# Second layer of a decoder kernel: GpSimd adds the exponentials of each pair of key tiles, and TensorE multiplies the sums of pairs with ones

## The chip, the core and the metric

The kernel runs on one core of a Trainium2 chip. Of its engines five matter here: TensorE (PE; its weight loads are shown as PEld) multiplies, VectorE (DVE) and ScalarE (ACT) empty PSUM and do the elementwise work, GpSimd (POOL) can work on SBUF beside them, SyncE (SP) issues transfers. The metric is the device time of one launch in microseconds (us), the median of several runs.

## The reference, cut to what matters

Three layers follow each other: attention with quantised numbers, cross attention, and attention with experts. Only the second is touched. There 16 sequences of 224 rows look at a context of 750 rows each, with 16 heads of 32 columns:

```python
q = (Q @ Wq + bq).reshape(B, L, H, E)
k = (K @ Wk + bk).reshape(B, S, H, E)
v = (V @ Wv + bv).reshape(B, S, H, E)
scores = jnp.einsum('blhe,bshe->bhls', q, k)
A = jax.nn.softmax(scale * scores, axis=-1)
out = jnp.einsum('bhls,bshd->blhd', A, v).reshape(B, L, H * E)
return out @ We + be
```

The softmax needs, for each row and head, the sum of the exponentials over all 750 keys.

## The kernel before, in words

The second layer handles one sequence (a "batch", `NB` = 16) after another, and in it four groups of four heads (`NG2` = 4, `GH` = 4). The 750 keys are six tiles of 125 (`MC`), taken as three pairs (`TP` = 3). For group g and pair t the work is a ring over four PSUM banks:

- `scores(u, g, t)`: TensorE writes the scores of two key tiles, four heads and 224 rows, keys on the partitions; the second half of it adds minus the row maximum.
- ScalarE's exponential `S.activation(prob[:, t, ...], ...)` (L1348) turns 1792 scores per partition into `prob`.
- `row_max(m, u, g, i)`: TensorE writes a quarter of the scores of the NEXT group into the same four banks, rows on the partitions, and VectorE's `reduce_max` (L1375) takes their maximum. Only then may the next `scores` write there (`r_free`).
- `values(u, g, t)`: TensorE multiplies `prob` with v and, in the other half of the same PSUM bank, with ones, which gives the sums of exponentials (L1239). Four heads stand side by side in the array, each in 32 of its columns.

After the third pair VectorE's `attend` takes the reciprocal of the sums and multiplies (L1387, L1388). `combine` (L1380 to L1382) turns the four maxima of the next group into the bf16 numbers that the small transposes of unit M (L1147) need, and M must be done before the first `scores` of the next group.

Between these steps TensorE fills its time with the dense work of the next batch, by the table `SLOTS`: slot 2t+1 lies behind `scores(t)`, slot 2t+2 behind `row_max(t+1)`, slot 0 at the group's start. Slot 4 is empty in groups 1, 2 and 3. In group 0 the units are transposes of the context (C) and the output product (O) of the batch before; in groups 1 to 3 they are the q, k and v products (Q, K, VV; L1137 to L1139). The order of a group on TensorE is: `row_max` 0 of the next group, M, slot 0, then for t = 0, 1, 2: `scores`, slot, `row_max` t+1, slot, `values`. Each engine runs its own program in order and waits on semaphores; the first and the last batch are written out, the fourteen between are a loop of seven rounds of two batches. GpSimd only adds the bias `be` to the rows of each batch (L1130). In the last batch there is no dense work left except O.

Of the kernel before, what the change touches and what calls it, by code (L numbers as in the profile page):

```python
# [6 lines left out]
F32 = mybir.dt.float32  # L7
# [5 lines left out]
ALU = mybir.AluOpType  # L13
# [8 lines left out]
NB, NS, D = 16, 224, 512  # L22
# [6 lines left out]
NCTX, MT = 750, 6  # L29
MC = NCTX // MT  # L30
H2, DH2 = 16, 32
# [44 lines left out]
def decoder_kernel(nc, a, out):  # L76

    V, S, G, PE = nc.vector, nc.scalar, nc.gpsimd, nc.tensor
    ctx = ExitStack()
    with ctx:  # L80
        arenas = []

        def open_arena(name, size, st):
            arenas.append((st.enter_context(nc.sbuf_tensor(name, [P, size // 4], F32)), {"low": 0, "high": size}))
            st.callback(arenas.pop)

        def own(name, shape, dt=F32, st=ctx):

            return st.enter_context(nc.sbuf_tensor(name, shape, dt))
# [23 lines left out]
        def ps(name, shape, dt=F32, st=ctx):  # L113
            return st.enter_context(nc.psum_tensor(name, shape, dt))
# [18 lines left out]
        ones = own("ones", [P, P])  # L133
# [8 lines left out]
        psum = ps("psum", [P, 8, D])  # L142
# [796 lines left out]
        L2 = ExitStack()  # L939
        SCALE2 = 1.0 / math.sqrt(DH2)  # L940
        GH = P // DH2
        NG2 = H2 // GH
        NK = NCTX + 2
        HC = NK // 2
        TP = MT // 2
# [2 lines left out]
        Wl = {n: own(f"W{n}_rest", [P, KC, D], F32R, L2) for n in "qkv"}  # L948
        ctxT_h, ctxT_l = (own("ctx_T_" + n, [P, KC, NK], F32R, L2) for n in ("high", "rest"))
        x1T_h, x1T_l = (own("x1_T_" + n, [P, KC, NS], F32R, L2) for n in ("high", "rest"))  # L950
        open_arena("arena_2", 122 * 1024, L2)
        We = sb("We", [P, KC, D], F32, L2)
        bias = sb("bias_qk_by_partition", [P, 2, NG2], F32, L2)
        bvT = sb("bias_v_by_partition", [P, KC], F32, L2)
# [12 lines left out]
        vR = sb("v_rows", [MC, 2, MT, D], F32, L2)  # L967
# [37 lines left out]

        ctx_r = sb("ctx_rows", [MC, MT, D], F32, L2)
        prob = sb("exps_by_key", [MC, TP, GH, 2 * NS], F32, L2)


        C, Q, K, VV, O, M = "ctx", "q", "k", "v", "out", "max"  # L1010
# [33 lines left out]
            return ORDER[at], 1  # L1044

        with phase(nc, "x2", "c", "x", "y0", "y1", "yb", "cmm", "chi", "clo", "qmm", "qmv", "kmm", "kmv", "vmm", "vmv", "rmm", "rfr", "nmx", "tmm", "tmv",
                   "smm", "exp", "avm", "att", "omm", "ord", "dch", "st") as (
                ctx_in, x_in, y_in0, y_in1, y_ready, c_mm, c_high, c_rest, q_mm, q_moved, k_mm, k_moved, v_mm, v_moved, r_mm, r_free, nmx_ready, t_mm, t_moved,
                s_mm, exp_done, av_mm, attended, o_mm, o_read, dch, r2_out), nc.Block() as block:
            y_in = (y_in0, y_in1)  # L1050

            def loop(eng, first, body, final):
# [9 lines left out]
            def y_count(b, u):  # L1062
                return b * 8 + (16 if u == 0 else 8)

            def score_psum(n, cols):
                return psum[0:n, 0:GH, 0:cols]
# [57 lines left out]
            @block.gpsimd  # L1124
            def _(pool):
                with pool.Fori(0, NB // 2) as pair:
                    for u in range(2):
                        b = pair * 2 + u
                        pool.wait_ge(y_in[u], y_count(b, u))
                        G.tensor_tensor(y2[:, u, :, :], y2[:, u, :, :], be[:, :].unsqueeze(1).broadcast_to([HALF, 2, D]), ALU.add).then_inc(y_ready, 1)  # L1130

            @block.tensor
            def _(pe):
# [98 lines left out]
                def values(u, g, t):  # L1232
                    for s in range(2):
                        mt = 2 * t + s
                        for to in range(2):
                            for j in range(GH):
                                h = g * GH + j
                                lhsT = vR[:, u, mt, h * DH2:(h + 1) * DH2] if to == 0 else ones[0:MC, 0:DH2]
                                last = PE.matmul(psum[DH2 * j:DH2 * (j + 1), 6 + g % 2, to * NS:(to + 1) * NS], lhsT, prob[:, t, j, s * NS:(s + 1) * NS],  # L1239
                                                 start=(mt == 0 and to == 0), stop=(mt == MT - 1 and to == 1))  # L1240
                    last.then_inc(av_mm, 1)

                def body(b, u, first, last):
                    b_next, b_before = b + 1, b - 1 if not first else None
                    for g in range(NG2):
                        n = b * NG2 + g
                        more = not (last and g == NG2 - 1)
                        g_r, u_r = (g + 1) % NG2, u if g < NG2 - 1 else 1 - u

                        def slot(i):  # L1250
                            for what in SLOTS[g][i]:
                                dense(what, b, b_next, b_before, u, first, last)

                        def next_max(i):
                            if not more:
                                return
                            if i == 0:
                                pe.wait_ge(q_moved, n + 2)
                                pe.wait_ge(k_moved, n * 2 + 4)
                                pe.wait_ge(r_free, n * 4 + 4)  # L1260
                            else:
                                pe.wait_ge(exp_done, n * TP + i)
                            row_max(n + 1, u_r, g_r, i)

                        def next_scores(t):
                            if more:
                                pe.wait_ge(r_free, n * 4 + (4 + t + 1))
                            elif t == 0:
                                pe.wait_ge(r_free, n * 4 + 4)
                            else:  # L1270
                                pe.wait_ge(exp_done, n * TP + t)
                            if t == 0:
                                pe.wait_ge(t_moved, n + 1)
                            scores(u, g, t)

                        def next_values(t):
                            if t == 0:
                                pe.wait_ge(attended, n + 1)
                                if g == 0:
                                    pe.wait_ge(v_moved, b * MT + MT)  # L1280
                            pe.wait_ge(exp_done, n * TP + (t + 1))
                            values(u, g, t)
                        next_max(0)
                        dense((M, g), b, b_next, b_before, u, first, last)
                        slot(0)
                        for t in range(TP):
                            next_scores(t)
                            slot(2 * t + 1)
                            next_max(t + 1)
                            slot(2 * t + 2)  # L1290
                            next_values(t)
# [12 lines left out]
                        row_max(0, 0, 0, i)  # L1304

                def final():
                    for i in range(2):
                        if i == 0:
                            pe.wait_ge(o_read, 2 * NB - 2)
                            pe.wait_ge(t_moved, NB * NG2)  # L1310
                        unit(O, i, 4 + i, NB - 1, 1)
# [3 lines left out]
            def _(act):  # L1315
# [19 lines left out]
                def body(b, u, first, last):  # L1335
                    for g in range(NG2):
                        n = b * NG2 + g

                        def slot(i):
                            for what in SLOTS[g][i]:  # L1340
                                if present(what, first, last):
                                    unit(*what, bank(what), b + 1, 1 - u)
                        unit(M, g, bank((M, g)), b, u)
                        slot(0)
                        for t in range(TP):
                            act.wait_ge(s_mm, n * TP + (t + 1))
                            act.wait_ge(av_mm, n * TP + (t + 1))
                            S.activation(prob[:, t, :, :], score_psum(MC, 2 * NS), ACT.Exp, scale=SCALE2).then_inc(exp_done, 1)  # L1348
                            slot(2 * t + 1)
                            slot(2 * t + 2)  # L1350
# [7 lines left out]
            def _(dve):  # L1358
# [24 lines left out]

                def attend(n, g, ch):

                    dve.wait_ge(av_mm, n * TP + 2 * TP)
                    ch.link(V.reciprocal(inv[:, :], psum[:, 6 + g % 2, NS:2 * NS]))  # L1387
                    V.tensor_tensor(o2T[:, g, :], psum[:, 6 + g % 2, 0:NS], inv[:, :], ALU.mult).then_inc(attended, 1)  # L1388

# [28 lines left out]

                def first():
                    dve.sem_inc(av_mm, TP)  # L1420
                    dve.sem_inc(attended, 2)
                    for i, (kind, j) in enumerate(FIRST):
                        unit(kind, j, 4 + i % 2, 0, 0)
                    for i in range(4):
                        reduce_max(0, i)
                    combine(0, Chain(dve, dch))
# [837 lines left out]
```

## Time and profile before

| | |
|---|---|
| median of 3 runs | 5535.03 us (5529.34 to 5535.2) |
| the profiled execution | 5532.44 us, its span 5530.6 us |
| TensorE busy over the span | 3949.7 us (71%) |
| VectorE, ScalarE, GpSimd busy | 2808.5 (51%), 1760.4 (32%), 250.3 (5%) |
| second layer's loop over batches | first `values` at 1625.3 us, last at 3306.5 us |

The page gives shares over three layers with different limits, so the numbers of use are those of the second layer alone. A row of the profile counts each float32 product as two matmul instructions: the 1536 products with v and the 1536 with ones appear as 3072 each. "Busy" of TensorE is time in which at least one matmul is in flight; starts that follow each other tell its pace.

### The profile page before, as it was taken

To read this page: it belongs to the slowest core of one execution; us is meant where nothing else is said; L and a number is where in the kernel's file an instruction comes from. 1 tells how busy PE (TensorE), PEld (TensorE's weight loads), DVE (VectorE), ACT (ScalarE), POOL (GpSimd) and SP (SyncE) were. 2 spreads that over 40 slices of the span, in tenths; PEclk is the share of its full clock that TensorE was granted. 3 is DMA by queue.
4 is the path that set the end of the run, shared out by engine and by line. 5 is a ranking of instruction groups with operands and counts; after the bars stand their busy time and mean duration, and the time that the engine had idled before them with its cause. 6 is when DMAs were issued, how large, how long until landed. Compare 5 with 4: busy or idle time off the path is not lost. (4 is left out here: it accounts for less than half of the span.)

```text
span 5530.6 us, 86185 instructions
## 1 busy us (share of the span) xinstructions
PE 3949.7 (71%) x31789; PEld 2779.0 (50%) x31819; DVE 2808.5 (51%) x4238; ACT 1760.4 (32%) x3704; POOL 250.3 (5%) x298
## 2 busy tenths in 40 slices
PE   0499411395069999999999972888835499999970
PEld 0234211262056666666666642555525388887860
DVE  6666988897524343344444335777773122223324
ACT  0105079782023333333333320444421122222310
POOL 0000000000000000000000000000001300000113
PEclk9999555556579999999999985999975699999985
DMA  3001423231210010001001002000001222222213
GB/s 118 0 0 48 111 76 87 78 96 62 85 51 22 23 40 27 22 23 44 22 23 38 14 5 83 0 0 0 0 0 54 85 68 68 68 68 68 71 51 129
DMA packets 156416, 266.34 MB, mean 48 GB/s; under 512 B 75824, under 2 KB 75824, under 8 KB 155264
## 3 DMA queue, kind: packets, MB, share of 16 engines
q1 hardware_dynamic: 143488, 229.39, 13.0%
q0 software_dynamic: 12672, 33.07, 2.1%
q8 instruction: 218, 3.57, 0.3%
q14 instruction: 38, 0.31, 0.0%
HBM read 165.11 MB, written 67.96 MB: 42 GB/s over the span
## 5 line engine op out<-in xcount | busy, mean ns | idle before, releaser
L1375 DVE TENSOR_REDUCE arena<-psum 112x4 f32<-112x1504 f32 x256 | 441.4, 1724 | 887.5 <-PE psum L1216 886.0
L1348 ACT ACTIVATE arena<-psum 125x1792 f32<-125x1792 f32 x192 | 320.0, 1667 | 423.9 <-PE psum L1229 423.9
L2062 PE MATMUL psum<-tokens_T_high,w_high 128*128 128x224 f32 x1280 | 357.4, 279 | 29.0 <-PE psum L2064 15.2
L543 PE MATMUL psum<-arena 64*112 64x224 bf16 x1024 | 127.2, 400 | 348.6 <-DVEq L652 261.2
L2063 PE MATMUL psum<-tokens_T_rest,w_high 128*128 128x224 f32 x1280 | 354.0, 277 | 0.0
L2064 PE MATMUL psum<-tokens_T_high,w_rest 128*128 128x224 f32 x1280 | 352.9, 276 | 0.0
L668 ACT ACTIVATE arena<-arena,scales 112x224 bf16<-112x224 int8 x512 | 286.0, 559 | 35.1 <-DVEq L653 35.0
L2140 ACT ACTIVATE arena<-psum 128x448 f32<-128x448 f32 x160 | 87.0, 544 | 633.8 <-PE psum L2064 633.8
L2181 DVE TENSOR_TENSOR gelu_T_rest<-arena,gelu_T_high 128x448 fp32r<-128x448 f32 x160 | 100.0, 625 | 369.1 <-ACT gelu_T_high L2145 369.1
L1216 PE MATMUL psum<-arena 32*112 32x376 f32 x2048 | 243.8, 532 | 60.8 <-issue 26.6
L543 PEld LDWEIGHTS psum<-arena 64*112 64x112 bf16 x1024 | 81.7, 200 | 394.2 <-DVEq L652 283.6
L2062 PEld LDWEIGHTS psum<-tokens_T_high,w_high 128*128 128x128 f32 x1280 | 248.4, 194 | 46.3 <-issue 46.3
L2062 PE MATMUL psum<-w_high,gelu_T_high 128*112 128x512 f32 x640 | 255.4, 399 | 12.4 <-PE psum L2053 11.3
L417 PE MATMUL psum<-arena 128*128 128x512 bf16 x1104 | 251.2, 383 | 13.8 <-DVEq L457 8.0
L2064 PE MATMUL psum<-w_high,gelu_T_rest 128*112 128x512 f32 x640 | 252.3, 394 | 0.0
L2063 PE MATMUL psum<-w_rest,gelu_T_high 128*112 128x512 f32 x640 | 251.9, 394 | 0.0
L2064 PEld LDWEIGHTS psum<-tokens_T_high,w_rest 128*128 128x128 f32 x1280 | 248.6, 194 | 0.0
L2063 PEld LDWEIGHTS psum<-tokens_T_rest,w_high 128*128 128x128 f32 x1280 | 248.5, 194 | 0.0
L2191 DVE COPY arena<-psum 112x512 f32<-112x512 f32 x80 | 55.3, 692 | 345.3 <-PE psum L2064 345.3
L1239 PE MATMUL psum<-arena 125*32 125x224 f32 x3072 | 224.8, 365 | 5.4 <-ACT arena L1348 5.4
L1225 PE MATMUL psum<-arena 32*125 32x224 f32 x3072 | 209.0, 388 | 19.0 <-DVE arena L1375 18.4
L1239 PE MATMUL psum<-arena,ones 125*32 125x224 f32 x3072 | 221.5, 361 | 0.0
(296 smaller groups left out, 8696.2 us busy)
## 6 DMA issues: line engine op xcount, KB each, us to landing
arena<-L_ffn_moe_w SPq DMA_DIRECT2D x16, 2048.0 KB, 12.0
arena<-arena SPq DMA_DIRECT2D x32, 896.0 KB, 6.1
arena<-ctx SPq DMA_DIRECT2D x16, 1500.0 KB
expert_rows<-arena SPq DMA_DIRECT2D x40, 448.0 KB, 3.1
arena<-x SPq DMA_DIRECT2D x2, 7168.0 KB, 22.8
arena<-x_after_attn SPq DMA_DIRECT2D x32, 448.0 KB, 15.3
dots_ints<-arena SPq DMA_DIRECT2D x16, 784.0 KB, 4.8
arena<-dots_ints SPq DMA_DIRECT2D x16, 784.0 KB, 5.6
```

The source lines that it names most:

```text
L417: last = PE.matmul(psum[:, j, :], qkvw_q[:, k, bass.ts(oc, P)], hT[:, k, j * D:(j + 1) * D], start=(k == 0), stop=(k == KC - 1))
L543: last = PE.matmul(psum[0:HALF, 4 * (hg % 2) + j, half * NS:(half + 1) * NS], stage[at, u, h // 2, half * HALF:(half + 1) * HALF], stage[a ...
L668: last = S.activation(junk[:, hg % 2, j, :], d8[:, u, h, (j % 2) * NS:(j % 2 + 1) * NS], ACT.Exp, bias=col("lowest")[0:HALF], scale=col("m ...
L1216: last = PE.matmul(psum[0:HALF, j, 0:HC], qT[rows, u, g, half * HALF:(half + 1) * HALF], kT[rows, u, g, c * HC:(c + 1) * HC], start=True, ...
L1225: PE.matmul(psum[0:MC, j, s * NS:(s + 1) * NS], kT[rows, u, g, keys], qT[rows, u, g, :], start=(s == 0), stop=False)
L1239: last = PE.matmul(psum[DH2 * j:DH2 * (j + 1), 6 + g % 2, to * NS:(to + 1) * NS], lhsT, prob[:, t, j, s * NS:(s + 1) * NS], start=(mt == 0 ...
L1348: S.activation(prob[:, t, :, :], score_psum(MC, 2 * NS), ACT.Exp, scale=SCALE2).then_inc(exp_done, 1)
L1375: return V.tensor_reduce(rmx[:, i // 2, i % 2, :], score_psum(HALF, HC), axis=AX.X, op=ALU.max).then_inc(r_free, 1)
L2062: PE.matmul(to, wh(k), xh(k), start=(k == 0), stop=False)
L2063: PE.matmul(to, wh(k), xl(k), start=False, stop=False)
L2064: last = PE.matmul(to, wl(k), xh(k), start=False, stop=(k == n - 1))
L2181: V.tensor_tensor(gTl[:, 2 * j:2 * j + 2, :], gT[:, j % 2, :, :], gTh[:, 2 * j:2 * j + 2, :].bitcast(F32), ALU.subtract).then_inc(g_rest, 1)
```

## The change

GpSimd gets new work: as soon as the exponentials of pair t are there, it adds the two key tiles of the pair into a new tile `pair2` (125 partitions x 896 floats). TensorE multiplies ones with `pair2` instead of with both halves of `prob`, in a function of its own, `sums`. It does so one step later than before: the sums of pair t stand behind the values of pair t+1, and those of the last pair stand in the next group, behind slot 0 and ahead of its first `scores`. `attend` waits for the sums. The exponential of the next group waits until GpSimd has read `prob`.

```diff
+                        for g in range(NG2):
+                            for t in range(TP):
+                                i = (b * NG2 + g) * TP + t
+                                pool.wait_ge(exp_done, i + 1)
+                                pool.wait_ge(sum_mm, i + 1)
+                                G.tensor_tensor(pair2[:, t, :, :], prob[:, t, :, 0:NS], prob[:, t, :, NS:2 * NS], ALU.add).then_inc(paired, 1)
...
-                        for to in range(2):
-                            for j in range(GH):
-                                h = g * GH + j
-                                lhsT = vR[:, u, mt, h * DH2:(h + 1) * DH2] if to == 0 else ones[0:MC, 0:DH2]
-                                last = PE.matmul(psum[DH2 * j:DH2 * (j + 1), 6 + g % 2, to * NS:(to + 1) * NS], lhsT, prob[:, t, j, s * NS:(s + 1) * NS],
-                                                 start=(mt == 0 and to == 0), stop=(mt == MT - 1 and to == 1))
+                        for j in range(GH):
+                            h = g * GH + j
+                            last = PE.matmul(psum[DH2 * j:DH2 * (j + 1), 6 + g % 2, 0:NS], vR[:, u, mt, h * DH2:(h + 1) * DH2],
+                                             prob[:, t, j, s * NS:(s + 1) * NS], start=(mt == 0), stop=False)
                     last.then_inc(av_mm, 1)
+
+                def sums(n, g, t):
+                    pe.wait_ge(paired, n * TP + (t + 1 + TP))
+                    for j in range(GH):
+                        last = PE.matmul(psum[DH2 * j:DH2 * (j + 1), 6 + g % 2, NS:2 * NS], ones[0:MC, 0:DH2], pair2[:, t, j, :],
+                                         start=False, stop=(t == TP - 1))
+                    last.then_inc(sum_mm, 1)
...
                             values(u, g, t)
+                            if t >= 1:
+                                sums(n, g, t - 1)
...
                         slot(0)
+                        if not (first and g == 0):
+                            sums(n - 1, (g - 1) % NG2, TP - 1)
...
                             act.wait_ge(av_mm, n * TP + (t + 1))
+                            act.wait_ge(paired, n * TP + (t + 1))
...
-                    dve.wait_ge(av_mm, n * TP + 2 * TP)
+                    dve.wait_ge(sum_mm, n * TP + 2 * TP)
```

TensorE at the end of a group, from the last values to the transposes of M, before (here each product is one row entry; `x2_exp` is set by the exponential, `x2_rfr` by `reduce_max`, `x2_qmv` and `x2_kmv` when q and k have left PSUM):

```order
L1239 MATMUL psum<-arena 32x224 [waits x2_exp]
L1239 MATMUL psum<-arena 32x224 x3
L1239 MATMUL psum<-arena,ones 32x224 x4
L1239 MATMUL psum<-arena 32x224 x4
L1239 MATMUL psum<-arena,ones 32x224 x4
L1216 MATMUL psum<-arena 112x376 [waits x2_rfr,x2_kmv,x2_qmv]
```

The same place in the changed kernel (`x2_ps` is set by GpSimd's addition):

```order
L1244 MATMUL psum<-arena 32x224 [waits x2_exp]
L1244 MATMUL psum<-arena 32x224 x7
L1251 MATMUL psum<-arena,ones 32x224 [waits x2_ps]
L1251 MATMUL psum<-arena,ones 32x224 x3
L1223 MATMUL psum<-arena 112x376 [waits x2_rfr,x2_kmv,x2_qmv]
```

Of sixteen products twelve are left, and the four with ones stand last, behind a wait of their own.

TensorE ahead of the first `scores` of group 2, in the changed kernel; the first two rows are the end of slot 0:

```order
L1145 MATMUL psum<-ctx_T_rest,Wk_high 128x376
L1146 MATMUL psum<-ctx_T_high,Wk_rest 128x376
L1251 MATMUL psum<-arena,ones 32x224 [waits x2_ps]
L1251 MATMUL psum<-arena,ones 32x224 x3
L1232 MATMUL psum<-arena 125x224 [waits x2_tmv,x2_rfr]
```

Before, the `scores` stood directly behind slot 0; now the four products of the group before stand between them.

GpSimd at the start of a batch in the changed kernel (`x2_y0`: rows of the batch are loaded; `x2_sum`: TensorE has read `pair2`):

```order
L1131 TENSOR_TENSOR arena<-arena 112x1024 [waits x2_y0]
L1135 ISA
L1137 TENSOR_TENSOR arena<-arena 125x896 [waits x2_sum,x2_exp]
L1135 REGISTER_ALU
L1137 TENSOR_TENSOR arena<-arena 125x896 [waits x2_sum,x2_exp]
```

Twelve such additions follow each bias addition, where there was none.

## Rows read from the trace of the kernel before

**Rows 1.** One stretch: us, busy PE, PEld, DVE, ACT, POOL; clock, DMA share, GB/s

```profile
2000.00:2500.00 500.00, 481.26 (x5013) 323.16 (x5009) 206.16 (x226) 166.90 (x203) 9.54 (x4) 0.99 0.10 28
```

**Rows 2.** Groups of instructions by line: the products in values

```profile
L1239 PE MATMUL psum<-arena 125*32 125x224 f32 x3072 | 224.8, 365 | 5.4 <-ACT arena L1348 5.4
L1239 PE MATMUL psum<-arena,ones 125*32 125x224 f32 x3072 | 221.5, 361 | 0.0
```

**Rows 3.** Waits in 1625 to 3307: us in total, times, longest

```profile
PE psum L1225 <- DVE arena L1375: 18.4, 57, 1.6
```

**Rows 4.** Timeline (start, us), group 2, pair 1: reduce, next scores

```profile
1999.35 1.72 DVE L1375 TENSOR_REDUCE arena<-psum 112x4 f32<-112x1504 f32 x1 [5.71 <-PE psum L1216]
...
2001.12 1.04 PE L1225 MATMUL psum<-arena 32*125 32x224 f32 x16 [0.20 <-DVE arena L1375]
```

**Rows 5.** Timeline, group 3, pair 0: reduce, last two chunks of values, next scores

```profile
2018.23 1.73 DVE L1375 TENSOR_REDUCE arena<-psum 112x4 f32<-112x1504 f32 x1 [3.66 <-PE psum L1216]
...
2020.40 0.56 PE L1239 MATMUL psum<-arena 125*32 125x224 f32 x8
2020.78 0.56 PE L1239 MATMUL psum<-arena,ones 125*32 125x224 f32 x8
2021.27 1.04 PE L1225 MATMUL psum<-arena 32*125 32x224 f32 x16
```

**Rows 6.** Timeline, start of group 3: reduce of row_max 0, first scores

```profile
2010.95 1.73 DVE L1375 TENSOR_REDUCE arena<-psum 112x4 f32<-112x1504 f32 x1 [2.36 <-PE psum L1216]
...
2013.14 1.04 PE L1225 MATMUL psum<-arena 32*125 32x224 f32 x16
```

**Rows 7.** Timeline, a group 0 from its first scores into group 1

```profile
2039.07 1.04 PE L1225 MATMUL psum<-arena 32*125 32x224 f32 x16 [0.56 <-DVE arena L1375]
...
2043.69 1.72 DVE L1375 TENSOR_REDUCE arena<-psum 112x4 f32<-112x1504 f32 x1
...
2045.47 0.85 PE L1225 MATMUL psum<-arena 32*125 32x224 f32 x12
...
2051.21 1.72 DVE L1375 TENSOR_REDUCE arena<-psum 112x4 f32<-112x1504 f32 x1 [0.17 <-PE psum L1216]
...
2053.30 1.04 PE L1225 MATMUL psum<-arena 32*125 32x224 f32 x16
...
2054.57 1.66 ACT L1348 ACTIVATE arena<-psum 125x1792 f32<-125x1792 f32 x1 [2.17 <-PE psum L1229]
...
2062.16 0.19 DVE L1382 SCALAR_TENSOR_TENSOR arena<-arena 112x8 bf16<-112x8 f32 x1
2062.44 1.73 DVE L1375 TENSOR_REDUCE arena<-psum 112x4 f32<-112x1504 f32 x1
2062.50 0.26 PE L1147 MATMUL psum<-identb,arena 112*128 112x112 bf16 x2
...
2064.22 1.04 PE L1225 MATMUL psum<-arena 32*125 32x224 f32 x16
```

**Rows 8.** A loop jump: the timeline's first row_max behind it, first scores

```profile
1928.38 0.89 PE L1216 MATMUL psum<-arena 32*112 32x376 f32 x4 [2.52 <-issue]
...
1934.40 1.87 PE L1225 MATMUL psum<-arena 32*125 32x224 f32 x16
```

**Rows 9.** Timeline, the last batch, group 0, pair 0: reduce, next scores

```profile
3221.84 1.72 DVE L1375 TENSOR_REDUCE arena<-psum 112x4 f32<-112x1504 f32 x1 [2.83 <-PE psum L1216]
...
3224.84 0.75 PE L1225 MATMUL psum<-arena 32*125 32x224 f32 x4
```

**Rows 10.** Additions and L1365 by line (total us, mean ns), then both on the timeline

```profile
L1130 POOL TENSOR_TENSOR arena<-arena 112x1024 f32<-112x1024 f32 x16 | 38.1, 2386 | 1714.1 <-DMA arena<-x_after_attn 1714.1
...
L1365 DVE TENSOR_TENSOR ctx_T_rest<-psum,ctx_T_high 128x500 fp32r<-128x500 f32 x96 | 62.7, 673 | 37.5 <-ACT ctx_T_high L1323 36.6
...
1552.77 4.67 POOL L1130 TENSOR_TENSOR arena<-arena 112x1024 f32<-112x1024 f32 x2 [162.71 <-DMA arena<-x_after_attn]
...
1554.50 0.68 DVE L1365 TENSOR_TENSOR ctx_T_rest<-psum,ctx_T_high 128x500 fp32r<-128x500 f32 x1 [0.97 <-ACT ctx_T_high L1323]
```

More of the change, by code:

```diff
@@ L950, in decoder_kernel @@
         x1T_h, x1T_l = (own("x1_T_" + n, [P, KC, NS], F32R, L2) for n in ("high", "rest"))
-        open_arena("arena_2", 122 * 1024, L2)
+        open_arena("arena_2", 127 * 1024, L2)
         We = sb("We", [P, KC, D], F32, L2)
@@ L1007, in decoder_kernel @@
         prob = sb("exps_by_key", [MC, TP, GH, 2 * NS], F32, L2)
+        pair2 = sb("exps_of_key_pairs", [MC, TP, GH, NS], F32, L2)
         C, Q, K, VV, O, M = "ctx", "q", "k", "v", "out", "max"
@@ L1046, in decoder_kernel @@
         with phase(nc, "x2", "c", "x", "y0", "y1", "yb", "cmm", "chi", "clo", "qmm", "qmv", "kmm", "kmv", "vmm", "vmv", "rmm", "rfr", "nmx", "tmm", "tmv",
-                   "smm", "exp", "avm", "att", "omm", "ord", "dch", "st") as (
+                   "smm", "exp", "ps", "sum", "avm", "att", "omm", "ord", "dch", "st") as (
                 ctx_in, x_in, y_in0, y_in1, y_ready, c_mm, c_high, c_rest, q_mm, q_moved, k_mm, k_moved, v_mm, v_moved, r_mm, r_free, nmx_ready, t_mm, t_moved,
-                s_mm, exp_done, av_mm, attended, o_mm, o_read, dch, r2_out), nc.Block() as block:
+                s_mm, exp_done, paired, sum_mm, av_mm, attended, o_mm, o_read, dch, r2_out), nc.Block() as block:
             y_in = (y_in0, y_in1)
@@ L1306, in final @@
                 def final():
+                    sums(NB * NG2 - 1, NG2 - 1, TP - 1)
                     for i in range(2):
@@ L1420, in first @@
                     dve.sem_inc(av_mm, TP)
+                    dve.sem_inc(sum_mm, TP)
+                    dve.sem_inc(paired, TP)
                     dve.sem_inc(attended, 2)
```

## The prediction

> **What bounds the kernel now.** I first cut the second layer out of the span, since the page's shares mix three layers. In 500 us of its loop TensorE has a matmul in flight for 481 us, VectorE is busy 206, ScalarE 167 and GpSimd under 10, at a granted clock of 0.99 [rows 1]. So TensorE's pace looks like the limit and GpSimd is free. The groups by line then say what the change can touch: the products with ones are 3072 instructions, as many as those with v, and half of them go [rows 2]. The list of waits says that TensorE is not alone, though: 57 times `scores` waited for VectorE's `reduce_max`, 18.4 us in all [rows 3]. The timeline shows where, and it decides the sum: a saving counts only where the next step on TensorE is not held by VectorE.
>
> **The unit.** One chunk of 8 matmul instructions (four heads side by side) starts 0.38 us behind the one ahead of it (2020.40 to 2020.78), and the last chunk of `values` is followed by `scores` after 0.49, so 0.11 is the change of the array's shape [rows 5]. A block of `values` has four chunks. The change removes six chunks with ones per group and adds three. Three chunks x 0.38 x 64 groups = 73 us is the most that TensorE can give back. By place: `values(0)` loses two chunks (0.76), `values(1)` with `sums(0)` and `values(2)` with `sums(1)` lose one each (0.38), and one chunk moves behind slot 0 of the next group, where it costs 0.38 plus one more change of shape, 0.49. `sums` behind `values` needs no change of shape.
>
> **Walk through one batch.** An interval can shrink until `scores` starts 0.05 behind the end of the reduce, the least distance in rows (2064.17 to 2064.22) [rows 7].
>
> Groups 1 to 3, pair 0: the reduce ends at 2019.96, `scores` starts at 2021.27, slack 1.31 - 0.05, more than 0.76. All of 0.76 counts, three times [rows 5].
>
> Groups 1 to 3, pair 1: slot 4 is empty, only `values` covers the reduce. It ends at 2001.07 and `scores` already waits 0.20 for it [rows 4]. Nothing is saved here, the wait grows from 0.20 to 0.58. These are 45 of the 57 waits (three groups x 15 batches; 45 x 0.20 = 9 of the 18.4 us) [rows 3].
>
> Groups 1 to 3, pair 2: a dense unit and `values` lie behind `row_max` 3; VectorE has been waiting 2.36 us when the next `row_max` comes [rows 6]. All of 0.38 counts, three times.
>
> Boundaries 1 to 2 and 2 to 3: the reduce ends at 2012.68, `scores` starts at 2013.14 because slot 0 ends only then [rows 6]. The added chunk is on the path: -0.49 each.
>
> Group 0, pair 0: reduce ends 2045.41, `scores` 2045.47. Saved: nothing. Pair 1: reduce ends 2052.93, `scores` 2053.30: 0.32 counts. Pair 2: M starts at 2062.50, held by VectorE's chain that ends with L1382 at 2062.35, which starts from the last transposes and not from `values`. Saved: nothing. Boundary 0 to 1: `scores` comes at 2064.22, TensorE and the reduce (2064.17) ready together, so the chunk costs 0.44 to 0.49; I take 0.45 [rows 7].
>
> Boundary 3 to 0: `scores` waited 0.56 for the reduce [rows 7]; a chunk and a change of shape fit in: 0. Behind the seven loop jumps it is otherwise: after 2.52 us without an instruction TensorE works at half rate, the `scores` that follow show 1.87 where others show 1.04 [rows 8]. There the chunk takes about 0.75 and the wait is nearly gone, so I put 0.75 on each jump.
>
> Per batch: 3 x 0.76 + 3 x 0.38 + 0.32 - 0.45 - 2 x 0.49 = 2.31. Fifteen batches: 34.7. Jumps: 7 x 0.75 = -5.3. The last batch runs mostly at half rate, with slack of 1.28 behind its first block of `values` (3223.56 to 3224.84) [rows 9]; with four to five blocks like that it gives 0 to 6, less about 1 us at the end, where the last sums wait for GpSimd with nothing to hide it. I take +4. Sum: 33 us.
>
> **What the new work costs.** GpSimd's addition is nearest to its bias addition: 2386 ns for 1024 elements per partition, so 896 take about 2.1 us [rows 10]; 192 of them are 400 us over 1680. The tightest user is the last pair of group 0: its exponential ends at 2056.23, its sums are wanted at about 2064.2, 8 us later, against 2.2 needed [rows 7]. In front of the first pair of a batch GpSimd now also has the bias addition, 2.4 more, and that pair's sums are wanted about 10 us behind its exponential. GpSimd's queue holds no one else: rows of a batch are loaded tens of us before. ScalarE's new wait looks one whole group back. `attend` now starts behind slot 0, 1 to 2 us later than before, and takes 1.9; the next reduce comes about 4 us behind `scores`. None of this is on the path. A satisfied wait ahead of `sums` has no row of its own; its cost lies between 0 and 0.11 (as if it were another change of shape). The `scores` of rows 5 stand behind a satisfied wait and a change of shape, and both together make 0.11 [rows 5]; so I take 0 for the wait alone. At 0.11 on the six places per batch where it would count (three of pair 2, three boundaries) it would be 10 us.
>
> **The number.** The sum is made against the profiled execution, 5532.4 us, which lies 2.6 under the median of 5535.0. 5535 - 33 gives 5502; since the wait is more likely to be free and the last batch could give more than I booked, I keep 5501.
>
> **Rivals.**
> (a) The forecast, gain 27 to 42 us, 5493 to 5508: 0.60.
> (b) VectorE doesn't hold `scores` back, all of the chunks count: 73 less 64 x 0.11 for the added shapes, 66 us, 5469. For it: TensorE is 96% busy. Against: the 45 waits where nothing hides the reduce. With gains from 45 us on: 0.06.
> (c) `sums` costs more than its chunk, by its wait or by the shape of the array. At 0.11 each the gain is some 23 us, 5512; at twice that, 13 and 5522. For it: no row shows a chunk with a wait of its own inside a block. Gain 11 to 27: 0.19.
> (d) No difference (within 11 us, 0.2%, about what a measurement of this kernel tells from no change): the ring of `scores`, exponential, `row_max` and reduce binds more places than I counted, for instance pair 0 of groups 1 to 3. Without those 3 x 0.76 nothing is left of the 2.31 per batch. The slack of 1.31 there speaks against it [rows 5]. 0.09.
> (e) Slower: GpSimd's addition holds VectorE off SBUF or PSUM for its 2.1 us. In group 0 the pair 0 addition would lie from about 2042.1 to 2044.2, across the L1365 subtractions and the reduce at 2043.69: 1.3 us lost. In groups 1 to 3 pair 0's reduce would start 0.8 late with 0.5 of slack left: 0.3 each. With what pairs 1 and 2 of group 0 add, some 2.8 us per batch, 16 x 2.8 = 45, so 5547. It decides from 2.3 us per batch. Against it: two bias additions ran from 1552.77 to 1557.44, and the L1365 inside took the same 0.68 as alone [rows 10]. 0.04.
> The Trainium skill's page "SBUF — State Buffer", section "Who interferes with whom", says that a VectorE instruction with two SBUF inputs and a GpSimd instruction that reads SBUF exclude each other for the whole instruction, and one with a single SBUF input does not. By that rule L1365 and the reduces go free, as the row shows for L1365, but L1380 and L1382 do not; the bias addition, now behind the last pair of group 3, would hold them about 1.4 us, just inside the time until M, and the sum would stay as it is. No row here has such a meeting.
> (f) Slower: TensorE waits longer in group 0 and its clock falls there as behind the loop jumps. Six us at half rate cost 3 us; 14 times that are 42, and 5543. Against: it already stands 0.56 and 0.76 us in that stretch at full clock, and the half rate came only behind 2.5 us of standing and in the last batch [rows 7 to 9]. The longest wait would become about 0.8. 0.02.
>
> The range 5487 to 5523 takes (a) whole, most of (c) and the rim of (b). Faster by over 0.2%: (a), (b), (c) = 0.85. Same: 0.09. Slower: 0.06.
>
> **What would show it.** In the profile after, a chunk with ones should appear 768 times as 4 products (1536 instructions), half of the busy time of today. `scores` of pair 1 in groups 1 to 3 should wait 0.5 to 0.6 us for the reduce, that of pair 0 in group 0 about 0.8; the waits of `scores` for VectorE should add up to about 18 + 15 x (3 x 0.38 + 0.7) = 46 us instead of 18. From one batch's group 0 to the next it should take 2.3 us less than today (about 1.6 less across a loop jump). GpSimd's rows should read 2.0 to 2.2 us, and no one should wait for GpSimd except at the very end. I would be wrong if TensorE waits for GpSimd in the loop, if L1365 or the reduces are longer, if the half-rate stretches spread beyond the jumps, or if the gap ahead of `sums` is over 0.1 us.

## The result and the profile after

The changed kernel takes 5478.41 us (median of 4 runs, 5477.24 to 5486.33), the kernel before 5532.18 in the same comparison: ratio 0.9906, 95% interval 0.9892 to 0.992. That is 54 us where I had forecast 33, and below 5487, the low end of my range. Two rows of the page after, the span and the busy time by engine:

```profile
span 5475.4 us, 83861 instructions
...
PE 3870.9 (71%) x30253; PEld 2713.8 (50%) x30283; DVE 2829.8 (52%) x4238; ACT 1760.5 (32%) x3704; POOL 654.2 (12%) x490
```

The span is 55.2 us shorter (5530.6 to 5475.4). The groups by line and the list of waits for the second layer (us in total, times, longest), which answer to [rows 2, 3, 10]:

```profile
L1137 POOL TENSOR_TENSOR arena<-arena 125x896 f32<-125x896 f32 x192 | 401.8, 2092 | 1255.1 <-ACT arena L1366 1255.1
...
L1244 PE MATMUL psum<-arena 125*32 125x224 f32 x3072 | 187.4, 362 | 5.4 <-ACT arena L1366 5.4
...
L1251 PE MATMUL psum<-arena,ones 125*32 125x224 f32 x1536 | 111.5, 363 | 0.8 <-POOL arena L1137 0.8
...
L1398 DVE TENSOR_TENSOR arena<-arena 112x8 f32<-112x8 f32 x64 | 28.8, 450 | 1.7
```

```profile
PE psum L1232 <- DVE arena L1393: 42.8, 67, 1.1
PE psum L1251 <- POOL arena L1137: 0.8, 1, 0.8
```

The addition takes 2092 ns (I had 2.1 us), the products with ones are halved, `scores` now waits 42.8 us for VectorE instead of 18.4 (I had 46), and TensorE waits for GpSimd once, at the very end. A group 2, pair 1 on the timeline (start, us), which answers to [rows 4]:

```profile
1989.52 2.10 POOL L1137 TENSOR_TENSOR arena<-arena 125x896 f32<-125x896 f32 x1 [5.33 <-ACT arena L1366]
1989.91 0.90 PE L1223 MATMUL psum<-arena 32*112 32x376 f32 x8
1990.74 0.96 PE L1244 MATMUL psum<-arena 125*32 125x224 f32 x16
1990.88 1.72 DVE L1393 TENSOR_REDUCE arena<-psum 112x4 f32<-112x1504 f32 x1 [4.94 <-PE psum L1223]
1991.52 0.56 PE L1251 MATMUL psum<-arena,ones 125*32 125x224 f32 x8
1992.65 0.66 PE L1232 MATMUL psum<-arena 32*125 32x224 f32 x8 [0.57 <-DVE arena L1393]
```

Note the 0.57 at the last row: one chunk is gone and the wait for the reduce took its place, as foreseen. Pair 2 of group 0 went as foreseen too: there the transposes M now wait about 0.50 us for VectorE's L1400, once in each batch but the first (8.3 us in 15 waits, the last one longer).

So the steps of the walk are there, and the sum is still off. To find where, I took the starts of the small transposes M of all 64 groups from both traces. From the M of group 3 to that of the next group 3 across a plain batch it is 103.80 us before (2010.82 to 2114.62) and 101.70 after (2001.97 to 2103.67): 2.10 less, forecast 2.31. Fifteen times that is 31.5. A back jump is the branch from the end of the loop's body to its start, the jump's target; seven rounds make six of them. The two groups around a back jump of TensorE's loop are longer than plain ones by 6.8 to 7.5 us before and by 2.6 to 5.4 after; over all six jumps 42.9 us before and 23.9 after. That is 19.0 more, and I had put -5.3 there. The rest of the 55.2, above all the last batch, gives 4.7 (forecast +4). The rows at one jump, before and then after:

```profile
1928.38 0.89 PE L1216 MATMUL psum<-arena 32*112 32x376 f32 x4 [2.52 <-issue]
1930.90 1.60 PE L1216 MATMUL psum<-arena 32*112 32x376 f32 x4 [1.63 <-issue]
```

```profile
1922.76 1.61 PE L1223 MATMUL psum<-arena 32*112 32x376 f32 x8 [2.86 <-issue]
1924.31 0.37 PE L1154 MATMUL psum<-identb,arena 112*128 112x112 bf16 x2
```

The times in brackets, 2.52, 1.63 and 2.86, are stretches in which TensorE has no instruction and waits for nothing that the profile shows; I call one a stand. Before, `row_max` stands, runs 4 of its 8 matmuls, stands a second time and goes on at half rate (1.60 for what took 0.89; the granted clock from 1930.90 to 1934.40 is 0.50). After, there is one stand. It is so at all six jumps: 2.5 to 2.9 and then 1.6 to 1.9 us before, a single stand of 2.6 to 3.0 us after. Nothing in the diff is about that.

### The profile page after: what moved, and what is told of

Read it like the earlier page. It is cut to its first block and busy times, and to the rows that moved or that the text cites. A ratio compares the mean times of both kernels' runs of the same rounds, so it can differ in the third digit from the quotient of the medians.

```text
span 5475.4 us, 83861 instructions
## 1 busy us (share of the span) xinstructions
PE 3870.9 (71%) x30253; PEld 2713.8 (50%) x30283; DVE 2829.8 (52%) x4238; ACT 1760.5 (32%) x3704; POOL 654.2 (12%) x490
## 5 line engine op out<-in xcount | busy, mean ns | idle before, releaser
L1393 DVE TENSOR_REDUCE arena<-psum 112x4 f32<-112x1504 f32 x256 | 441.4, 1724 | 768.7 <-PE psum L1223 768.6
L1137 POOL TENSOR_TENSOR arena<-arena 125x896 f32<-125x896 f32 x192 | 401.8, 2092 | 1255.1 <-ACT arena L1366 1255.1
L1232 PE MATMUL psum<-arena 32*125 32x224 f32 x3072 | 203.4, 380 | 43.2 <-DVE arena L1393 42.8
L1232 PEld LDWEIGHTS psum<-arena 32*125 32x125 f32 x3072 | 134.7, 186 | 120.5 <-DVE arena L1393 84.3
```

Of the source, the lines that this page charges most:

```text
L1137: G.tensor_tensor(pair2[:, t, :, :], prob[:, t, :, 0:NS], prob[:, t, :, NS:2 * NS], ALU.add).then_inc(paired, 1)
L1232: PE.matmul(psum[0:MC, j, s * NS:(s + 1) * NS], kT[rows, u, g, keys], qT[rows, u, g, :], start=(s == 0), stop=False)
L1393: return V.tensor_reduce(rmx[:, i // 2, i % 2, :], score_psum(HALF, HC), axis=AX.X, op=ALU.max).then_inc(r_free, 1)
```

## Experiments

My theory A: the second stand is a matter of where the jump lands. It says that after a back jump TensorE has to fetch its program anew, in blocks, and that where the target lies a few instructions ahead of a block's end, a second fetch is paid in series. The change takes some 200 instructions out ahead of the loop (52 products of float32, four instructions each), and so moved the target by accident. Theory B: the change's own work makes the jump cheaper. Theory C: the granted clock alone makes the difference. The Trainium skill's page "Runtime: NRT & Kernel Launch", section "Instruction fetch mechanics", says that programs come in 16 KiB blocks of 256 instructions and that a taken branch out of the blocks at hand waits for the target's block; it has no cost for it. The stand of 2.5 us and the second one behind it are this case's rows; no row shows a fetch, so that a stand is a fetch stays an inference.

### The target moved, 32 and 208 instructions

Both add small matmuls to an unused bank, ahead of the second layer's loop, where TensorE stands for the weights anyway (16 in the kernel before, 104 in the changed one; each is two instructions, a weight load and a matmul):

```diff
                 def _(pe):
+                    for _ in range(16):
+                        PE.matmul(psum[0:16, 1, 0:16], identb[:, 0:16], identb[:, 0:16], start=True, stop=True)
                     pe.wait_ge(w_in, 16 * 8)
```

> The kernel before, with 32 more instructions (16 matmuls of 16x16 into an unused bank) on TensorE while it waits for the weights of the second layer, so that all of its later program lies 32 instructions further on. Theory A (place in the program): the kernel before pays two program fetches in series at each of its six back jumps, because the jump lands a few instructions ahead of the end of a block of program (it runs four products and then stands again, 1.63 us); 32 instructions further the second stand goes. Six jumps cost 43 us beyond the normal pace in the kernel before and 24 in the changed one, so this kernel should come out near 5515 (5509 to 5521), with one stand of 2.5 to 3 us at each jump. Theory B (the change's own work makes the jumps cheaper, by shorter values or by the later sums): nothing moves, 5530 to 5534, two stands at each jump. Theory C (the difference lies in the states of the clock alone): two stands remain, and only the half-rate stretch varies.

Measured: 5509.9 us (5508.3 to 5512.9), the kernel before 5532.7 beside it, ratio 0.9961 (0.9947 to 0.9975). The six jumps cost 21.2 us instead of 42.9, the plain batch 103.79 as before. TensorE at the same jump as above:

```profile
1925.67 0.56 PE L1241 MATMUL psum<-arena,ones 125*32 125x224 f32 x8
1928.75 0.90 PE L1218 MATMUL psum<-arena 32*112 32x376 f32 x8 [2.52 <-issue]
1929.59 0.27 PE L1149 MATMUL psum<-identb,arena 112*128 112x112 bf16 x2
```

One stand, no half rate in `row_max`. Instructions that compute nothing made the kernel before 23 us faster. Theory B can't explain that, and theory C, by which two stands remain, falls as well.

> The changed kernel with 208 more instructions (104 small matmuls) on TensorE in the same place; its program in front of the loop is about 208 instructions shorter than that of before, so this puts the jump's target back to where it was in its block. Theory A: the second stand is back, 5478 + 17 = 5495 (5489 to 5501), and the difference to the kernel before falls to the 33 to 38 us of my walk through the batch. Theory B: nothing moves, 5476 to 5482.

Measured: 5510.9 us (5507.4 to 5512.4), ratio to before 0.9961 (0.9947 to 0.9975). The second stand is back and splits `row_max` after the same four matmuls:

```profile
1925.79 1.59 PE L1225 MATMUL psum<-arena 32*112 32x376 f32 x4 [4.21 <-issue]
1928.55 1.60 PE L1225 MATMUL psum<-arena 32*112 32x376 f32 x4 [1.17 <-issue]
```

The time misses my 5495 (5489 to 5501), and the difference to the kernel before is 21.8 us instead of 33 to 38. The jumps cost 53.6 us, 11 more than in the kernel before: at the jump shown the first stand is 4.21 instead of 2.52 and both halves run at half rate. Over the six jumps the first stand is 4.0 to 4.2 five times and 2.95 once, so its length varies from jump to jump in one and the same program. The plain batch stays at 101.70. So the place decides about the second stand; the first one's length has a cause of its own. The padding moves the jump instruction as well as its target. That the target decides is argued from the second stand, which comes four matmuls behind it in both kernels.

### Other displacements, and GpSimd's jump

> The changed kernel (loop kept) with 96 more instructions (48 small matmuls) ahead of the second layer on TensorE. If the place of the jump's target in its block of program decides, 96 is too little to bring it near the block's end: one stand per jump, six jumps cost 24 us beyond the pace (20 to 28) and the time is 5478 to 5483. If any displacement costs, it lies about halfway to a_pad208, 38 us.

Measured (one run): 5478.9 us, jumps 23.2 us.

> The same with 240 more instructions. The target now lies just behind the start of the next block: one stand per jump again, 20 to 28 us over six jumps, 5480 to 5486, though more is added than in a_pad208. If the cost grows with what is added, it is above the 54 us of a_pad208.

Measured (one run): 5477.1 us, jumps 24.3 us. With 0, 96, 208 and 240 instructions added, the jumps cost 23.9, 23.2, 53.6 and 24.3: neither the amount nor any displacement does it; of these four places one is bad.

a_pad208_pool is a_pad208 with GpSimd's loop written out:

```diff
-                with pool.Fori(0, NB // 2) as pair:
+                for pair in range(NB // 2):
                     for u in range(2):
```

> a_pad208 with GpSimd's loop over batches written out as well, TensorE's loop kept. a_pad208 paid 54 us at the six jumps, 11 more than the kernel before with the same two stands. If that is GpSimd's own jump, whose program is fetched at the same moment now that its loop body is longer, it falls to 43 (40 to 46). If it is TensorE's own layout (where the jump itself stands in its block), it stays at 51 to 56.

Measured (one run): 5512.6 us, jumps 53.5 us. GpSimd's own jump has no part in it. The first stand is 4.1 to 4.4 us at four jumps here and 2.6 at two; what makes it so long in this layout stays open.

### No jump at all

```diff
-                loop(pe, first, body, final)
+                first()
+                body(0, 0, True, False)
+                for b in range(1, NB - 1):
+                    body(b, b % 2, False, False)
+                body(NB - 1, 1, False, True)
+                final()
```

> The kernel before with TensorE's loop over batches written out (the other engines keep theirs): no jump on TensorE. Both theories: the 43 us of the six jumps go, 5489 (5485 to 5495), if a written-out program is fetched ahead without a stand.

Measured: 5490.9 us (5490.5 to 5492.2), ratio to before 0.9927 (0.991 to 0.9943). The 42 us of the jumps are gone.

> The changed kernel with TensorE's loop written out. Theory A: 5478 - 24 = 5454 (5449 to 5459), and the difference to the written-out kernel of before is the change's real worth, 33 to 38 us (15 batches of 2.1, and the last one). Theory B (the change makes more than that of work vanish): the difference stays near 54 without any jump.

Measured: 5455.9 us (5453.5 to 5457.7), ratio to before 0.9864 (0.9847 to 0.988). The groups around the former jumps are as long as any other (within 0.04 us). The difference of the two is 35.0 us: that is what the change itself is worth. The plain batch takes 103.80 us in b_unroll and 101.59 here, and 15 x 2.21 = 33 with the last batch gives the 35. The other 19 of the 54 us came from where the change happened to move the program.

The experiments below all have TensorE's loop written out, so that no back jump on TensorE plays a part, and compare with 5490.9 and 5455.9.

### GpSimd's additions alone

The kernel before, plus GpSimd's additions as in the changed kernel (without their wait for `sum_mm`) and ScalarE's wait for them; TensorE's work is that of before.

```diff
+                        for g in range(NG2):
+                            for t in range(TP):
+                                i = (b * NG2 + g) * TP + t
+                                pool.wait_ge(exp_done, i + 1)
+                                G.tensor_tensor(pair2[:, t, :, :], prob[:, t, :, 0:NS], prob[:, t, :, NS:2 * NS], ALU.add).then_inc(paired, 1)
...
                             act.wait_ge(av_mm, n * TP + (t + 1))
+                            act.wait_ge(paired, n * TP + (t + 1))
```

> The kernel before with TensorE's loop written out, and GpSimd's 192 additions of pairs beside it; nobody uses what they give, TensorE multiplies as before, ScalarE waits for them as in the changed kernel. So this is the cost of the new work by itself. Forecast's theory: nothing, 5491 as b_unroll (5488 to 5494). Rival (e), GpSimd holds VectorE off: up to 45 us more, 5536. By the rule of the port shared by VectorE and GpSimd, L1380 of group 3 waits about 1.2 us for the bias addition, with no effect on the end.

Measured: 5488.4 us (5484.9 to 5489.1), the plain batch 103.77 us against 103.80. Groups by line of this kernel, to be read beside [rows 10]:

```profile
L1387 DVE TENSOR_REDUCE arena<-psum 112x4 f32<-112x1504 f32 x256 | 441.2, 1724 | 828.5 <-PE psum L1222 827.2
L1136 POOL TENSOR_TENSOR arena<-arena 125x896 f32<-125x896 f32 x192 | 402.3, 2095 | 1266.3 <-ACT arena L1360 1266.3
...
L1377 DVE TENSOR_TENSOR ctx_T_rest<-psum,ctx_T_high 128x500 fp32r<-128x500 f32 x96 | 62.0, 671 | 31.9 <-ACT ctx_T_high L1334 31.9
```

402 us of GpSimd's work cost nothing, and neither the reduces (1724 ns) nor the subtractions (671 ns) are longer. Rival (e) falls.

### The order alone

`sums` multiplies ones with both halves of `prob`, GpSimd's additions are gone, ScalarE waits for `sum_mm`:

```diff
-                    pe.wait_ge(paired, n * TP + (t + 1 + TP))
-                    for j in range(GH):
-                        last = PE.matmul(psum[DH2 * j:DH2 * (j + 1), 6 + g % 2, NS:2 * NS], ones[0:MC, 0:DH2], pair2[:, t, j, :],
-                                         start=False, stop=(t == TP - 1))
+                    for s in range(2):
+                        for j in range(GH):
+                            last = PE.matmul(psum[DH2 * j:DH2 * (j + 1), 6 + g % 2, NS:2 * NS], ones[0:MC, 0:DH2], prob[:, t, j, s * NS:(s + 1) * NS],
+                                             start=False, stop=(t == TP - 1 and s == 1))
```

> The changed kernel with TensorE's loop written out, but sums multiplies ones with both halves of prob (two chunks for each pair) and GpSimd adds nothing. So only the order is the changed kernel's, the work is that of before. By the walk, against b_unroll per batch: pair 0 of groups 1 to 3 gives 3 x 0.76, boundaries 1 to 2, 2 to 3 and 0 to 1 cost 0.90 each, boundary 3 to 0 0.37: 0.8 slower per batch, 5491 + 12 = 5503 (5498 to 5508). Rival: the new order alone brings the gain, 5456.

Measured: 5494.3 us (5492.6 to 5496.7), 3.4 more than b_unroll; the plain batch takes 104.33 us, 0.53 more (I had 0.8). The order alone loses a little; the fewer chunks are the gain. The time is below my range (5498 to 5508); the direction is as expected, the loss is smaller.

### The delay by one pair

```diff
                             values(u, g, t)
-                            if t >= 1:
-                                sums(n, g, t - 1)
+                            sums(n, g, t)
```

and the two other calls of `sums` are left out.

> The changed kernel with TensorE's loop written out, each pair's sums directly behind its own values, none in the next group. By the rows GpSimd's sum is there 1 us before the values end even then, so nobody waits for GpSimd; pair 0 gives 0.38 less in three groups, and the three boundaries cost nothing instead of 0.52: 0.4 to 0.5 faster per batch, 5456 - 7 = 5449 (5445 to 5453). Rival: the delay by one pair was needed, TensorE waits for GpSimd 0.5 us or more at most of the 180 places, and it is slower, 5480 or more.

Measured: 5455.0 us (5451.6 to 5457.5), no better than a_unroll and above my range (5445 to 5453). But the plain batch takes 101.11 us, 0.48 less, as expected; from the first M to that of the last batch it gained 8.2 us. The last batch took that back. The stretch from the last batch's first M to a few us behind its end, in this kernel and then in a_unroll (the column behind the busy times is TensorE's granted clock). Up to the layer's last instruction on VectorE it is 106.6 and 96.2 us.

```profile
3131.61:3242.00 110.39, 77.68 (x708) 37.10 (x704) 34.45 (x35) 21.35 (x16) 24.99 (x12) 0.72 0.03 9
```

```profile
3140.69:3240.00 99.31, 67.39 (x716) 32.90 (x712) 34.57 (x35) 21.34 (x16) 25.00 (x12) 0.85 0.03 10
```

Two things come together there. TensorE's busy time is 77.68 against 67.39 us at a lower clock, 0.72 against 0.85. And in the last group, where no `row_max` and no reduce is left to cover GpSimd, the sums do wait for it, which I had not counted:

```profile
3209.00 1.72 PE L1244 MATMUL psum<-arena 125*32 125x224 f32 x16 [1.85 <-ACT arena L1367]
3211.07 0.97 PE L1251 MATMUL psum<-arena,ones 125*32 125x224 f32 x8 [0.35 <-POOL arena L1137]
3211.97 1.87 PE L1232 MATMUL psum<-arena 32*125 32x224 f32 x16
```

From the start of these `values` to the next `scores` it takes 2.97 us, and 3.07 at the next pair; in a_unroll, with the delay by one pair, 0.89 and 1.27. That is 3.9 us of the 10.4. Part of the 3.9 is the half rate, but even at the full rate GpSimd's sum comes 2.0 us behind the start of `values`, so most of it is the wait: the delay by one pair pays in the last group. How the rest divides between waits and clock, and why the clock is lower, stays open.

Inside the loop the delay was not needed: pair 0 of a group 1, GpSimd's addition and the products that use it,

```profile
2049.11 2.09 POOL L1137 TENSOR_TENSOR arena<-arena 125x896 f32<-125x896 f32 x1 [8.75 <-ACT arena L1367]
...
2051.89 0.96 PE L1244 MATMUL psum<-arena 125*32 125x224 f32 x16
2052.67 0.56 PE L1251 MATMUL psum<-arena,ones 125*32 125x224 f32 x8
```

The sum is there at 2051.20, its products start at 2052.67.

### The last sums into the wait

In groups 1 to 3 the last sums of the group before go behind `row_max` of pair 1; `attend` goes behind that reduce on VectorE.

```diff
-                        if not (first and g == 0):
+                        if g == 0 and not first:
                             sums(n - 1, (g - 1) % NG2, TP - 1)
...
                             slot(2 * t + 2)
+                            if g >= 1 and t == 1:
+                                sums(n - 1, g - 1, TP - 1)
                             next_values(t)
```

> The changed kernel with TensorE's loop written out; in groups 1 to 3 the last sums of the group before stand behind row_max of pair 1, where TensorE waits about 0.64 us for the reduce, instead of ahead of the first scores; attend goes behind that reduce on VectorE. If the walk is right, three boundaries win 0.52 each and pair 1 costs nothing: 1.5 per batch, 5456 - 22 = 5434 (5429 to 5440). Rival: the reduce of pair 1 is not what that step waits for, the chunk costs 0.4 there as elsewhere and nothing is won: 5452 to 5458.

Measured: 5432.6 us (5426.2 to 5435.1), ratio to before 0.9817 (0.9801 to 0.9833), 23 below a_unroll. The plain batch takes 99.97 us, 1.62 less than a_unroll's. `scores` of a group 1, pair 1 now:

```profile
2056.76 1.04 PE L1232 MATMUL psum<-arena 32*125 32x224 f32 x16 [0.19 <-DVE arena L1400]
```

The wait shrank from 0.57 to 0.19 and the chunk cost nothing there. So it is the reduce that the step waits for.

moved_two puts the second pair's sums there as well:

```diff
-                            if t >= 1:
-                                sums(n, g, t - 1)
+                            if t == 1:
+                                sums(n, g, 0)
...
                             if g >= 1 and t == 1:
+                                sums(n - 1, g - 1, TP - 2)
                                 sums(n - 1, g - 1, TP - 1)
```

> moved, with the second pair's sums of the group before placed there too (behind row_max of pair 1 in groups 1 to 3, behind slot 0 in group 0). In moved the step of pair 1 still waits about 0.27 us for the reduce, so a further chunk costs 0.12 there and saves 0.38 behind the values of pair 2; in group 0 it costs about 0.23 behind slot 0. Per batch 3 x 0.38 - 3 x 0.12 - 0.23 = 0.55: 5433 - 8 = 5425 (5419 to 5430), batch pace 99.4 us. Rival: GpSimd now waits for the reader of its tile and comes late, TensorE waits, 5433 or more.

Measured: 5422.5 us (5421.3 to 5425.7), ratio to before 0.9799 (0.9783 to 0.9816), the plain batch 99.45 us. The second chunk had only the rest of the wait to go into, as forecast: groups 1 to 3 gained 0.26 to 0.27 each and group 0 lost 0.27. It is the fastest version here, 112 us under the kernel before: 42 from the jumps, 35 from the change, the rest from these two moves.

## Why the prediction was wrong

**The unit and the walk** held, and with them the mechanism inside a batch. 0.38 per chunk and, between `values` and `scores`, 0.11 per change of shape reappear, and a satisfied wait ahead of `sums` costs nothing: the chunk behind `values` starts in the same pace. Pair 1 of groups 1 to 3 saved nothing, pair 0 and 2 all of theirs. The batch gave 2.10 instead of 2.31: the moved chunk cost 0.52 at each of three boundaries, where I had 0.49, 0.49 and 0.45, and 0.32 in group 0 came out as it was. That is 0.13 of the 0.21; the rest I can't place.

**The step that failed** is "Behind the seven loop jumps it is otherwise ... so I put 0.75 on each jump". It is the term "Jumps: 7 x 0.75 = -5.3". There are six back jumps, and I took their stands as a fixed part of the kernel and only asked what the moved chunk costs behind them. Instead of -5.3 the term was +19.0. The row with 2.52 us without an instruction was in my hands [rows 8], the second stand stood beside it in the timeline, and I asked neither what they are nor whether the change moves them. b_pad32 shows that 21.7 us of the kernel before hang on 32 instructions, a_pad208 that the changed kernel loses as much and more at the bad place. With one stand at each jump in both, the six cost 21.2 us without the change (b_pad32) and 23.9 with it. So the moved chunk, the only thing I had asked about, took some 2.7 us over six jumps, about 0.45 each for my 0.75 (a rough figure: the jumps of one kernel differ by up to 2.8 us), and the place gave 21.7.

**The last batch** gave 4.7 for my 4. This was luck as much as reading. From its first M to the start of the third layer the last batch took 107.5 us before and 102.7 after, but 106.1 in b_unroll and 103.3 in adds_only, which give TensorE the same work, and 105.1 in a_pad208, whose last batch is that of the changed kernel. What varies with such traces is as large as the term.

**GpSimd's cost** was right: nothing (adds_only). The meeting that the prediction named beside rival (e) was also seen, at the very place: the bias addition, now behind the last pair of group 3, and L1398, which reads two SBUF inputs (before, as L1380, 0.17):

```profile
1917.10 2.38 POOL L1131 TENSOR_TENSOR arena<-arena 112x1024 f32<-112x1024 f32 x1
1918.19 1.32 DVE L1398 TENSOR_TENSOR arena<-arena 112x8 f32<-112x8 f32 x1
```

It ends at 1919.51, when GpSimd ends (1919.48), 1.15 late. The Trainium skill's page "SBUF — State Buffer", section "Who interferes with whom", says that a VectorE instruction with two SBUF inputs contends with a GpSimd instruction that reads SBUF, and here the trace agrees. These rows lie ahead of a jump. In a plain batch L1398 took 1.40 us, the chain behind it ended at 2027.12 and M started at 2027.75, so it cost nothing, with 0.6 us to spare.

**The rivals:** (b), all chunks count, would have come near the measured time with the wrong cause; the waits of 42.8 us and the 35.0 us between b_unroll and a_unroll, where it wants 66, rule it out. (c) falls by the batch, (d) and (e) by a_unroll and adds_only, (f) by the clock of 1.00 in 2000 to 2500 us:

```profile
2000.00:2500.00 500.00, 474.98 (x4732) 315.00 (x4728) 217.85 (x231) 172.91 (x210) 133.25 (x63) 1.00 0.10 31
```

## What to carry to other kernels

Walk a pipelined ring step by step and let a saving count only until the next wait takes over; that gave the plain batch 2.31 us for a measured 2.10. (The forecast of 33 lies near the 35.0 of the written-out kernels only because its wrong term for the jumps, -5.3, offset other errors: without it the forecast is 38.7.) Before believing a difference of a few tenths of a per cent in a kernel with loops, look for stands without a releaser behind back jumps, count them in both kernels, and if they differ compare the two with the loop written out or padded. Work that has to be added on the bounding engine belongs where that engine waits: the first moved chunk was free there and had cost 0.52 elsewhere, the second cost about 0.12 instead of 0.38.

## What the runs showed of the hardware

- A back jump of TensorE's loop (two batches, some 4000 instructions) cost 3.5 to 4 us in the mean of six where one stand followed it (b_pad32 and the changed kernel), 7.1 with two stands (the kernel before), and 9 in one layout (a_pad208). The difference between the first and the second of these in the kernel before was 32 instructions of padding. Part of the cost is the half rate that follows a stand (1.60 us for what took 0.89).
- 402 us of GpSimd's float32 additions beside VectorE's reduces from PSUM and its subtractions with one SBUF input lengthened neither (1724 and 671 ns); an addition with two SBUF inputs was held 1.15 us, until GpSimd had ended. Over the layer L1398 went from a mean of 164 to 450 ns.
